# Cross attention: the projection's place between the two score pairs of a turn

## What is computed

```python
def xattn(target, source, target_mask, source_mask, Wq, bq, Wk, bk, Wv, bv):
    q = jnp.einsum('oc,bct->bot', Wq, target) + bq[None, :, None]      # 16 sequences, SIZE 256, T = S = 512
    k = jnp.einsum('oc,bcs->bos', Wk, source) + bk[None, :, None]
    v = jnp.einsum('oc,bcs->bos', Wv, source) + bv[None, :, None]
    q, k, v = (a.reshape(b, 16, 16, -1) for a in (q, k, v))            # 16 heads of 16 rows
    dot = jnp.einsum('bhdt,bhds->bhts', q, k) / math.sqrt(16)
    mask = target_mask[:, :, :, None] * source_mask[:, :, None, :]
    dot = mask * dot - (1.0 - mask) * 1000000.0
    amap = jax.nn.softmax(dot, axis=-1) * mask
    return jnp.einsum('bhts,bhds->bhdt', amap, v).reshape(b, 256, t)

x = x + attn(layernorm(x), ...)
x = x + xattn(layernorm(x), ctx, mask, mask, Wq, bq, Wk, bk, Wv, bv)
x = x + experts(layernorm(x), ...)
```

## Time and profile before

| | us |
|---|---|
| median of 3 runs | 2793.67 |
| lowest and highest run | 2780.36, 2794.4 |
| the profiled execution | 2779.66 |
| its span | 2778.2 |
| mean granted TensorE clock of the span | 0.975 |

### The profile page before, as it was taken

One profiled execution on the slowest core, in us unless ns is written; L12 is line 12 of the kernel. 1 busy time (PEld: TensorE's weight loads), 2 busy tenths in 40 slices (PEclk: granted clock), 3 DMA queues, 4 the chain that ended last, 5 costly groups with the idle time before them and its releaser, 6 DMA issues. The chain is left out here.

```text
span 2778.2 us, 51135 instructions
## 1 busy us (share of the span) xinstructions
PE 2603.6 (94%) x15536; PEld 1813.6 (65%) x15537; DVE 1869.1 (67%) x3829; ACT 1456.8 (52%) x2868; POOL 997.9 (36%) x1195
## 2 busy tenths in 40 slices
PE   7999999999999999999989999999998986399997
PEld 6888888888788888888733444444443422277775
DVE  6556655565544555444588888888887876677665
ACT  4334433344433344333457777777776764355554
POOL 2112211122211122111346656656655647333332
PEclk9999999999999999999989999999999997699999
DMA  4102222013212111112235555556555658655554
GB/s 152 67 9 75 75 75 75 12 64 137 80 46 74 42 60 60 48 43 72 70 91 123 133 137 138 140 130 139 129 136 119 143 146 294 223 106 107 106 106 84
DMA packets 144961, 282.49 MB, mean 102 GB/s; under 512 B 44016, under 2 KB 46960, under 8 KB 139760
## 3 DMA queue, kind: packets, MB, share of 16 engines
q1 hardware_dynamic: 116656, 214.20, 26.4%
q0 software_dynamic: 23664, 58.09, 10.0%
q10 hardware_dynamic: 4560, 9.18, 1.1%
HBM read 147.82 MB, written 81.68 MB: 83 GB/s over the span
## 5 line engine op out<-in xcount | busy, mean ns | idle before, releaser
L1768 DVE TENSOR_REDUCE b_negmax<-b_ps_s 128x2 f32<-128x1024 f32 x512 | 612.1, 1219 | 59.6 <-PE b_ps_s L1946 52.5
L298 POOL TENSOR_SCALAR probs<-probs,rinv 128x256 f32<-128x256 f32 x256 | 242.0, 945 | 1093.1 <-DVE rinv L482 1093.1
L1622 ACT ACTIVATE b_probs<-b_ps_s 128x1024 f32<-128x1024 f32 x512 | 520.5, 1021 | 193.7 <-PE b_ps_s L1957 192.6
L341 ACT ACTIVATE probs<-ps_s,negmax 128x128 f32<-128x128 f32 x256 | 94.2, 368 | 486.3 <-DVE negmax L475 486.3
L1970 PE MATMUL b_ps_o<-b_probs,b_v_stack 128*32 128x256 f32 (+1 forms) x2816 | 297.0, 494 | 0.9 <-ACT b_probs L1622 0.8
L1957 PEld LDWEIGHTS b_ps_s<-p_stack 56*128 56x128 f32 x1024 | 96.0, 184 | 275.5 <-issue 168.1
L1957 PE MATMUL b_ps_s<-p_stack 56*128 56x512 f32 x1024 | 257.7, 500 | 16.6 <-DVE b_negmax L1768 8.8
L1946 PE MATMUL b_ps_s<-p_stack 54*128 54x512 f32 x1024 | 226.6, 440 | 27.7 <-DVE b_negmax L1768 8.4
L602 PE MATMUL ps_proj<-xT_h,wq_h 128*128 128x512 f32 x512 | 216.8, 423 | 0.0
L2658 POOL DMA_INDIRECT out<-e_y,e_place_int x71 | 118.4, 1668 | 253.1 <-DMA out<-e_y,e_place_int 216.4
L602 PE MATMUL ps_proj<-xT_l,wq_h 128*128 128x512 f32 x512 | 201.4, 393 | 0.0
(11 more groups left out here) (354 smaller groups left out, 6631.5 us busy)
## 6 DMA issues: line engine op xcount, KB each, us to landing
p_stack<-b_split SPq DMA_DIRECT2D x168, 128.0 KB
p_stack<-p_split SPq DMA_DIRECT2D x162, 128.0 KB
e_row<-rows_by_expert SPq DMA_DIRECT2D x71, 258.0 KB, 2.9
b_out_tiles<-row_sum_inverses SPq DMA_DIRECT2D x64, 256.0 KB
x<-acc SPq DMA_DIRECT2D x15, 1024.0 KB, 5.0
x_in<-in_x SPq DMA_DIRECT2D x8, 1024.0 KB, 8.2
normalised_x_split<-xT_h SPq DMA_DIRECT2D x8, 1024.0 KB, 9.9
normalised_x_split<-xT_l SPq DMA_DIRECT2D x8, 1024.0 KB, 11.0
```

What stands on the lines that cost most here:

```text
L298: nc.gpsimd.tensor_scalar(probs[:, s, P:3 * P], probs[:, s, P:3 * P], rinv[:, s, 1:2], None, ALU.mult).then_inc(probs_done, 1)
L341: nc.scalar.activation(probs[:, s, 0:P], ps_s[s][:, 0:P], ACT.Exp, bias=negmax[:, s, 0:1], accum_out=rowsum[:, s, 0:1])
L1622: nc.scalar.activation(probs[:, k % 2, p, :, :], ps[:], ACT.Exp, scale=0.25).then_inc(e_done, 1)
L1768: nc.vector.tensor_reduce(negmax[:, k, p, :], ps[:], AX.X, ALU.max, negate=True).then_inc(m_reduced, 1)
```

## The change

On PE, in the turns that have a projection, `small_free` and `piece` move from the end of the turn, behind the second pair, into the branch p == 0, behind the values product and ahead of the second pair's E fill. The orders of the other engines aren't touched, nor is the choice of `parts`, nor the place of the transposes at k = 0. The last sequence has no projections.

```diff
--- before.py
+++ after.py
@@ -2013,12 +2013,12 @@
                                     values_product(g - 1, QUADS - 1, TBL - 1)
                                 if last:
                                     route_between(q, k, p)
+                                if piece_at((q, k), tail, last):
+                                    name, ahead = piece_at((q, k), tail, last)
+                                    small_free(where, name, ahead)
+                                    piece(where, b + ahead, name, ahead)
                         if parts == 2:
                             values_product(g + q, q, k - 1, 1, parts)
-                        if piece_at((q, k), tail, last):
-                            name, ahead = piece_at((q, k), tail, last)
-                            small_free(where, name, ahead)
-                            piece(where, b + ahead, name, ahead)
                         if k == 0 and not (last and q == QUADS - 1):
                             small_free(where, f"m{(q + 1) % QUADS}", (q + 1) // QUADS)
                             negmax_transpose(where, b + (q + 1) // QUADS, (q + 1) % QUADS)
```

## The result

The changed kernel takes 2847.51 us (median of 4 runs, 2845.13 to 2853.45), the kernel before beside it 2787.02 (4 runs, 2779.73 to 2794.4). The ratio is 1.0223, 95% interval 1.0202 to 1.0244: slower by 2.2%, 60.5 us. The two profiled executions lie further apart, 2853.45 against 2779.66, 73.8 us; of these, 72.7 lie between the first and the last E fill of the cross attention (953.8 against 881.2 us).

A forecast was written before the change was run, and what follows sets the result against it. PE was taken as the bound: 49.9 us of work in a 53.24 us sequence. 3.48 + 0.39 + 0.4 = 4.27 a sequence, 63.5 us in all on 2779.66, gave 2843; with run scatter 2848 was taken, range 2812 to 2866.

The forecast's parts named there:

- Step 1: Behind six projection turns a sequence, the next turn's first max-score fill waits 0.58 us for an exponential: 3.48 a sequence.
- E0': First exp-score fill on PE in the turn after a projection turn; forecast to start 0.34 us after the max-score fill before.
- M0': First max-score fill on PE in the turn after a projection turn; forecast to wait 0.58 us for an exponential.
- Step 2: In turn (2,3), a normalisation on ACT delays an exponential, so the second max-score fill waits 0.39 us more.
- M1: Second pair's max-score fill on PE in a turn; in a projection turn forecast to start 0.34 us after its exp-score fill.
- E1: Second pair's exp-score fill on PE in a turn; the max-score fill reusing its bank needs 1.59 us from its start.
- Step 3: At (1,0), a long maxima split on DVE delays transposes and an E fill: 0 to 0.8 us, 0.4 taken; (3,3): 0.
- Step 4: In (0,2), (0,3) and (2,2), the previous projection's raw copy ends 0.3 us before the next projection needs the bank: cost 0.
- Step 5: New neighbours on PE, such as values product then projection: plus or minus 0.1 us a turn, taken as 0.
- Absorption: New delays shrink PE's present waits; half of the 3.48 stays, the 0.39 and 0.4 vanish: 2806 to 2820, chance 0.13.
- Faster: DVE sets the pace and its waits for q projections vanish, so 19 us come back: 2761, chance 0.05.
- The clock's rival: Added PE waits bring every sequence's granted clock to 0.87: 112 us more, 2955, chance 0.02.

The follow-up runs named there:

- the swapped kernel: In projection turns, the projection stays behind the first pair and the whole values product moves behind the second, against the kernel before: 2806.96 us, ratio 1.0028.
- the run with half left behind: The changed kernel with half of each projection's matmuls behind the values product and half behind the second pair: 2809.17 us, ratio 1.0045 to the kernel before.
- half exponentials: The changed kernel with each exponential over half its columns, that half fed twice to the values product: 2857.36 us, ratio 1.0227 to the kernel before.
- the swap with the early copy: Whole values product behind the second pair, projection behind the first, DVE's projection copy between the two maxima: 2815.53 us, ratio 1.0058 to the kernel before.
- its base: The kernel before with each exponential over half its columns and that half fed twice to the values product: 2797.20 us, ratio 1.0027.

## Why the prediction was right, point by point

The forecast was 2848 with a range of 2812 to 2866; 2847.51 was measured, and the sum for the profiled execution, 2843, stands against 2853.45. That the medians agree to half a microsecond is luck: errors of several steps and the difference between median and profiled execution cancel in it.

*The bound.* PE's start-to-start sums, not its busy share, were the right view. Its waits went up by what the kernel lost, with a clock of 1.00 in an ordinary sequence.

*Step 1, what the gap hid.* Right in kind and place, and shown by experiment: filling the gap again with the values product, or with parts of the projection, takes the loss away in the order of the distance. The size was off by a fifth: 0.70 a gap instead of 0.58. The path is 1.61 and not 1.59, and the instruction behind a waiting M starts 0.43 after it instead of 0.33, which I hadn't counted. Six gaps make 4.2 and not 3.48. At (3,3) I missed that the slots turn round, so E0' and not M0' waits; the turns from (3,3) to (0,1) grew by 0.78 together.

*Step 2, the turn after v1.* Predicted 0.39. The turns (2,3) and (3,0) together grew by 0.91, 0.21 beyond a gap's 0.70. The wait is there: M1 of (2,3) starts 3.24 after the E1 at 1808.75, where 3.22 had been worked out. A part of it is given back in the next turn.

```profile
1808.75 0.50 PE L1957 MATMUL b_ps_s<-p_stack 56*128 56x512 f32 x2
...
1811.37 0.50 PE L1957 MATMUL b_ps_s<-p_stack 56*128 56x512 f32 x2
1811.99 0.50 PE L1946 MATMUL b_ps_s<-p_stack 54*128 54x512 f32 x2
```

*Step 3, DVE's chain at k = 3.* I took 0.4 between 0 and 0.8. Turns (1,0) and (1,1) together grew by 1.11, 0.41 beyond 0.70. The rows are those I had worked out, with DVE's long step:

```profile
1786.44 1.24 DVE L1775 TENSOR_TENSOR b_nm_split<-b_negmax,b_nm_split 128x16 fp32r<-128x16 f32 x1
...
1788.39 0.60 PE L1921 MATMUL b_ps_p<-p_ident,b_nm_split 128*8 128x128 f32 x4 [0.42 <-DVE p_raw_q L1750]
1789.52 0.50 PE L1957 MATMUL b_ps_s<-p_stack 56*128 56x512 f32 x2 [0.53 <-DVE b_negmax L1768]
```

The 0.42 and 0.53 are the 0.43 and 0.6 of that step; that they add up to 0.41 is since (1,1) became 0.58 shorter, its own wait on ACT being covered by them. The same trade showed when DVE was made faster. For (3,3) the prediction put nothing, since DVE's wait for the row sums wouldn't move. It did move: that wait is gone from the changed kernel's table.

*Step 4, the small bank.* Right: no projection waits for a copy in the changed kernel. In the swapped kernel, with the slack gone, it did, by the 0.36 that was worked out.

*Step 5, the seams.* In the changed kernel M1 to E0' takes 0.24 instead of the 0.33 from M to Pj, which is lost in the wait of M0', and no other seam shows. The bound itself was too low: two more seams a turn cost 0.21 in the run with half left behind.

*The sum.* 4.27 a sequence was forecast, the sum of the turns' medians gives 4.81 (2.12 in (0,2), (0,3) and (2,2), 0.78, 1.11 and 0.91 as above, less 0.11). Times 15 that is 72 us, the 73.7 between the two spans. The medians lie only 60.5 apart. The kernel before has the more runs above its fastest: 15 us in its first four, up to 34 us in the 21 runs beside the first experiments. Two things seen in the profiles do this, late stack loads and the product of the row sums that runs beside POOL. A longer sequence gives a load more time, and in the changed kernel's profile DVE waits for the row sums nowhere between 1500 and 2200 us, and the product behind them takes 0.17 or 0.18 us at (3,3) in every sequence; but they were seen in profiled executions alone, so that the changed kernel has fewer of them is argued and not shown. That I took 2848 and not 2843 rested on a scatter of the changed kernel over the same 14 us, and it scattered over 8 in its four runs.

*The rivals.* Absorption is refuted as a whole and true in part: where a new wait falls ahead of an old one ((1,1), (0,0), (3,0)), the old one shrinks, by 1.24 a sequence together. Faster: DVE's waits for projections did go, and nothing came of it. The clock's rival didn't happen in the changed kernel: 1.00 beside waits of 0.66. That holds against the rule of the Trainium skill, page "TensorE: Matmul & The Clock Gate", section "A second HAM failure mode: psum-queue depth-cycling", as quoted in the prediction. Two other runs show how near it was. With half exponentials the clock fell behind waits of 1.6 to 1.7, in seven of 14 sequences. In the swap with the early copy it fell behind two waits of 0.7 to 0.8 in a row, in four of 13. No length of a wait that decides it can be read from that.

## What to carry to other kernels

When work is moved from one gap to another, write down for both gaps which dependence crosses them and how long its path takes, from start to start: here 1.6 us had to pass between an E fill and the third fill after it, and it didn't matter whether a projection or a values product filled them. Where a fill waits for a reader of an earlier one, keep some long work in each gap between the pairs, and check by leaving a sixth and a half of it there that the loss follows the distance. Compare turns as well as totals: a shorter wait on one engine uncovers the next one, and several runs here gained 0.4 to 1.1 us in one turn and lost much of it, or more, in a later one.

## What the runs showed of the hardware

A DVE product, subtraction or cast of 16 columns that reads SBUF took mostly 0.17 to 0.25 us alone. Where it started while a POOL instruction on two tensors ran, it took up to 1.24 us, and 2.26 beside one of 2.39 (1751.32 in the earlier trace rows, 1786.44, 1762.13, 1766.21 and 1519.43 above). It ended 0.02 to 0.05 us after POOL's in most cases: 1519.43 + 2.26 is 1521.69, and 1519.28 + 2.39 is 1521.67. The Trainium skill, page "SBUF — State Buffer", section "SBUF: two separate sides", has it that DVE and GpSimd share a pair of ports as a lock, which a DVE instruction takes when it has two inputs in SBUF (against a GpSimd instruction that reads SBUF) or runs in a mode that uses both ports, and that the later one blocks. The trace agrees for the products and subtractions with two inputs from SBUF. The cast has one input, and took 0.97 and 1.02 us; the section names copies of 32-bit numbers from SBUF to SBUF as using both ports, which would cover it, but no run here shows the mode.

The granted clock fell to 0.50 behind a wait of 1.65 us in the run with half exponentials, where PE had been busy for 9.34 of the 10 us before 1788.00, and for 0.94 of the next 2 us. The same wait in the same turn of other sequences left it at 1.00 in seven of 14, and so did waits of 1.4 to 2.1 at (0,0) in eight of 12 sequences of its base. Two waits of 0.66 to 0.81 in a row brought it to 0.50 in four of 13 sequences of the swap with the early copy. Waits of 0.66, or of 0.42 and 0.53 in a row, left it at 1.00 in the changed kernel.

An instruction behind a waiting M fill starts 0.10 us later than without the wait (0.43 against 0.33), so a wait costs more than its own length. What fits is that the weight load of a waiting fill starts together with its matmul (both at 1781.18), where that of M1 had started at 1779.67, 0.23 ahead of it.
